# Attention and routed experts in one kernel: split weights held on chip, full tiles listed group by group

## The reference, cut to what matters

```python
x = x + _L0_xattn_ref(_layernorm(x), ctx, ctx, gates..., outnorm_scale)
xf = _layernorm(x).reshape(-1, 256)
top_w, top_i = jax.lax.top_k(softmax(xf @ router_w.T), 2)
comb = (top_w / sum(top_w)) scattered to [n, 8]
h = gelu(einsum('nc,ech->enh', xf, w1), approximate=False)
x = x + einsum('ne,enc->nc', comb, einsum('enh,ehc->enc', h, w2))
```

## Time and profile before

| | us |
|---|---|
| median of 3 executions (lowest, highest) | 728.24 (725.85, 734.26) |
| span of the profiled execution, first to last instruction | 716.1 |
| median less span: start and end that the span leaves out | 12.1 |
| TensorE busy | 616.2 (86% of the span) |
| VectorE, ScalarE, GpSimd busy | 402.2, 299.7, 256.9 |
| moved by DMA | 130.52 MB, mean 182 GB/s |

### The profile page before, as it was taken

One profiled execution on the slowest core, in us unless ns is written; L12 is line 12 of the kernel. 1 busy time (PEld: TensorE's weight loads), 2 busy tenths in 40 slices (PEclk: granted clock), 3 DMA queues, 4 the chain that ended last, 5 costly groups with the idle time before them and its releaser, 6 DMA issues.

```text
span 716.1 us, 18339 instructions
## 1 busy us (share of the span) xinstructions
PE 616.2 (86%) x5879; PEld 498.6 (70%) x5879; DVE 402.2 (56%) x1118; ACT 299.7 (42%) x582; POOL 256.9 (36%) x192
## 2 busy tenths in 40 slices
PE   2799988988999830099999999999999999999991
PEld 2578777776887730078787777777787878777880
DVE  1458678687686655045555555555555555555550
ACT  2444634625444200044545444444544454544440
POOL 0213148568475467012133232233231322312322
PEclk9965657557565555599999999999999999999996
DMA  9786486594541425913944938537649358377321
GB/s 313 272 323 224 173 292 223 208 329 176 196 185 75 177 81 178 367 26 54 343 101 102 349 48 260 179 59 222 218 74 369 56 135 298 52 205 243 48 36 22
DMA packets 58964, 130.52 MB, mean 182 GB/s; under 512 B 6384, under 2 KB 38384, under 8 KB 57904
## 3 DMA queue, kind: packets, MB, share of 16 engines
q1 hardware_dynamic: 44384, 110.91, 43.2%
q0 software_dynamic: 13392, 18.10, 14.1%
q10 hardware_dynamic: 1152, 1.07, 0.4%
HBM read 188.49 MB, written 40.13 MB: 319 GB/s over the span
## 4 chain that ended last, share of the span: by engine, by line
PE 69%; DVE 8%; ACT 6%; issue 5%; DMA 5%; POOL 4%; SPq 2%; POOLq 0%; DVEq 0%; ACTq 0%
PE bank L664 16%; PE bank L650 9%; PE bank L652 9%; PE bank L651 9%; PE bank L666 8%; PE bank L542 6%; PE bank L485 5%; DMA out<-ct,dst 2%; PE bank L634 2%; PE bank L527 2%; POOL rows L1282 2%; ACT xn L695 2%; DMA xrow<-rows 1%; POOL hrs L1274 1%; DVE rowb L874 1%
## 5 line engine op out<-in xcount | busy, mean ns | idle before, releaser
L650 PE MATMUL bank<-dt,wring 128*128 128x128 f16 x1136 | 198.5, 220 | 1.1 <-DVE dt L1201 1.1
L652 PE MATMUL bank<-dt,wring 128*128 128x128 f16 x1136 | 198.6, 220 | 0.0
L651 PE MATMUL bank<-dt,wring 128*128 128x128 f16 x1136 | 198.5, 220 | 0.0
L664 PE MATMUL bank<-wring,ct 128*128 128x512 f16 x568 | 192.3, 379 | 1.3 <-DVE ct L1217 1.3
L1217 DVE TENSOR_TENSOR ct<-dt,ct 128x512 f16<-128x512 f32 x142 | 98.3, 692 | 139.0 <-PE bank L666 113.1
L814 ACT ACTIVATE dt<-bank 128x512 f32<-128x512 f32 x142 | 84.8, 597 | 216.3 <-PE bank L652 216.3
L666 PE MATMUL bank<-wring,ct 128*128 128x256 f16 x568 | 154.8, 273 | 0.0
L1318 POOL DMA_INDIRECT out<-ct,dst x48 | 76.6, 1596 | 211.8 <-DMA out<-ct,dst 75.8
L650 PEld LDWEIGHTS bank<-dt,wring 128*128 128x128 f16 x1136 | 111.3, 98 | 25.1 <-issue 15.7
L651 PEld LDWEIGHTS bank<-dt,wring 128*128 128x128 f16 x1136 | 111.4, 98 | 0.9
L652 PEld LDWEIGHTS bank<-dt,wring 128*128 128x128 f16 x1136 | 111.4, 98 | 0.0
(11 more groups left out here) (139 smaller groups left out, 830.2 us busy)
## 6 DMA issues: line engine op xcount, KB each, us to landing
wring<-wsplit SPq DMA_DIRECT2D x284, 512.0 KB
wring<-in_w SPq DMA_DIRECT2D x16, 1024.0 KB, 12.0
xrow<-rows SPq DMA_DIRECT2D x71, 130.0 KB
wsplit<-wring SPq DMA_DIRECT2D x4, 2048.0 KB, 8.4
wsplit<-wcv SPq DMA_DIRECT2D x4, 2048.0 KB, 7.9
xa<-in_x SPq DMA_DIRECT2D x8, 512.0 KB, 9.1
kT<-in_ctx_t SPq DMA_DIRECT2D x8, 512.0 KB, 8.6
ctn<-in_ctx SPq DMA_DIRECT2D x8, 512.0 KB, 8.4
```

The costliest lines, as they stand in the source:

```text
L650: pe.matmul(o, hi, xT[k][:, c, :], start=(c == 0), stop=False)
L651: pe.matmul(o, hi, xT[k][:, CK + c, :], start=False, stop=False)
L652: mm = pe.matmul(o, lo, xT[k][:, c, :], start=False, stop=(c == CK - 1))
L664: pe.matmul(YP[k][:, 0:2 * D], gh[a][:, m4, :], wring[:, k, w:w + 2 * D], start=(a == 0 and m4 == 0), stop=False, skip_group_check=True)
```

## The change

The split weights of all eight experts lie in `wall` in SBUF; `wsplit`, the ring and its conditional loads are gone. The staging of an expert's fp32 numbers is in the part of `wall` that is not yet written (`first_stage`, `second_stage`). To make room, x isn't kept: it is loaded once for the first norm and again for the residual (`load_x_again`), and most buffers of the attention are single.

The order is new. A step t now has the whole of a group's attention and router in it (`w` = t), beside it `m` = t+1 (decay), `f` = t+2 (x, gates) and `r` = t-1 (ranks, scatter, list). It is cut into eight slots, and a slot may hold a tile: tile i runs in slot 4 of step 2 for i = 0, and so on, so that 44 tiles lie in steps 2 to 7, and 27 behind them. From group 1 on, each routed group gives a list of eight full tiles (`list_step`, 16 small steps on VectorE); the last gives 24 entries, with the ends that aren't full. Everything is unrolled; there is no loop and no value in a register for semaphores. The expert of a tile is taken from a word that packs eight of them, and the weights of each matmul are addressed by it.

Further: `output` has three matmuls of 256 columns in place of 512 and 256, with one sum in PSUM and one bank; ScalarE scales it (`weigh`) and makes the high part of the rows (`tile_high`); the sum on VectorE goes. A ring of three holds finished outputs (`YO`). The second norm goes from VectorE to ScalarE (`x1_norm`), the exponential of the router to GpSimd (`pow`). ScalarE changes its function table twice a step from step 3 on. The pad rows are written by SyncE.

```diff
-SPLIT = {e - 1: (e,) for e in range(NE)}
+SPLIT = {(-2, 7): (0,), (-1, 1): (1,), (-1, 2): (2,), (-1, 4): (3,), (-1, 6): (4,),
+         (0, 0): (5,), (0, 2): (6,), (0, 4): (7,), (0, 5): (8,), (0, 6): (9,), (0, 7): (10,),
+         (1, 0): (11,), (1, 2): (12,), (1, 4): (13,), (1, 6): (14,), (1, 7): (15,)}
...
+def tile_of(step, slot):
+    return PER * (step - 2) + slot - LAG
...
+        wall = sb("wall", [P, NE, 2 * (W1 + W2)], F16)
...
+        def steps(step):
+            for t in range(-2, NG + 1):
+                step(t, group(t), group(t + 1), group(t + 2), group(t - 1))
...
+            def load_rows(i):
+                if i % PER == 0 and i <= PER * (LAST - 1):
+                    sp.wait_ge(s_tab, 2 * (i // PER + 1))
+                    sp.wait_ge(s_sc, 16 * 2 * G * (i // PER + 2))
...
+            def expert(i):
+                if i // PER not in words:
+                    words[i // PER] = pe.value_load(word[0:1, i // PER:i // PER + 1], min_val=0, max_val=8 ** PER - 1)
+                return (words[i // PER] >> (3 * (i % PER))) & (NE - 1)
...
+            def weights(i, at, n):
+                return wall[:, bass.ds(experts[i], 1), at:at + n].rearrange("p o n -> p (o n)")
...
+                    if i == 0:
+                        pe.wait_ge(s_wl, 2 * NE)
+                        pe.wait_ge(s_wh, 2 * NE)
...
+                    experts[i] = pe.snap(expert(i), min_val=0, max_val=NE - 1)
...
+                        hi = weights(i, c * HID + m * P, P)
+                        lo = weights(i, W1 + c * HID + m * P, P)
+                        pe.matmul(o, hi, xT[i % XT][:, c, :], start=(c == 0), stop=False)
+                        pe.matmul(o, hi, xT[i % XT][:, CK + c, :], start=False, stop=False)
+                        mm = pe.matmul(o, lo, xT[i % XT][:, c, :], start=False, stop=(c == CK - 1))
...
-                    pe.matmul(YP[k][:, 0:2 * D], gh[a][:, m4, :], wring[:, k, w:w + 2 * D],
-                              start=(a == 0 and m4 == 0), stop=False, skip_group_check=True)
-                    mm = pe.matmul(YP[k][:, D:2 * D], gl[a][:, m4, :], wring[:, k, w:w + D],
-                                   start=False, stop=(a == 1 and m4 == 3), skip_group_check=True)
+                    pe.matmul(Y, gh[q][:, m4, :], weights(i, w, D), start=(a == 0 and m4 == 0), stop=False)
+                    pe.matmul(Y, gh[q][:, m4, :], weights(i, w + D, D), start=False, stop=False)
+                    mm = pe.matmul(Y, gl[q][:, m4, :], weights(i, w, D), start=False, stop=(a == 1 and m4 == 3))
...
+            def step(t, w, m, f, r):
+                if w is not None:
+                    logd(w, (0, 1, 2))
+                    scores(w, 0)
+                    logd(w, (3,))
+                for j in slots(t):
+                    i = tile_of(t, j)
+                    if live(i):
+                        hidden(i, 0)
+                    if live(i + 1):
+                        tile_turn(i + 1)
+                    if j == 0 and w is not None:
+                        scores(w, 1)
+                    if live(i - 1):
+                        output(i - 1, 0)
+                    if j == 0 and w is not None:
+                        values(w, 0)
...
+                    if j == 4 and f is not None:
+                        turn(f, 0)
+                        turn(f, 1)
+                    if j == 5 and w is not None:
+                        router_turn(w, 0)
+                    if j == 6 and w is not None:
+                        logits(w)
+                    if j == 7 and f is not None:
+                        gates(f)
+                    if live(i):
+                        hidden(i, 1)
+                    if j == 0 and w is not None:
+                        values(w, 1)
+                        values(w, 2)
+                    if live(i - 1):
+                        output(i - 1, 1)
...
+            def weigh(i):
+                act.wait_ge(s_m2, 2 * i + 2)
+                act.wait_ge(s_cw, i + 1)
+                after(act, s_oa, 16 * (i - YO + 1))
+                act.activation(yo[i % YO][:, :], Y, ACT.Copy, scale=cw[i % RW][:, :]).then_inc(s_yo, 1)
...
+                if w is not None:
+                    if t > 2:
+                        act.preload_act_table_set("natural_log_exp_and_others")
+                    floor(w)
+                    for b in range(G):
+                        decay(w, b)
+                if m is not None:
+                    log_sigmoid(m)
+                if w is not None and t > 1:
+                    act.preload_act_table_set("gelu_and_others")
...
+                    if j == 1 and r is not None:
+                        for b in range(G):
+                            scatter(r, b)
```

More of the change, by code:

```diff
@@ L71 @@
 B_MASK = B_IDENT + P
[L72 removed]
+B_TRI = B_MASK + P
 B_ONES = B_TRI + P
@@ L453, in _ @@
-            tiles(sp, tile)
+            load_c(0)
+            for half in range(3):
+                load_w(half)
+            def step(t, w, m, f, r):
+                if t == -2:
+                    load_x(1)
+                    load_x_again(0)
+                    load_k(1)
+                    for half in range(3, 7):
+                        load_w(half)
+                if t == -1:
+                    load_x(2)
+                    load_c(1)
+                    for half in range(7, 12):
+                        load_w(half)
+                    sp.dma_start(rows[SPARE:SPARE + P, :], pad_rows).then_inc(s_spare, 16)
+                    sp.dma_start(out[NT:NT + P, :], pad_rows[:, 0:D]).then_inc(s_spare, 16)
+                if t == 0:
+                    load_k(2)
+                    for half in range(12, 2 * NE):
+                        load_w(half)
+                if t == 1:
+                    load_x_again(1)
+                if t > 0 and f is not None:
+                    load_x(f)
+                for j in slots(t):
+                    i = tile_of(t, j)
+                    if live(i + 2):
+                        if i + 2 == PER * (LAST - 1):
+                            sp.wait_ge(s_pr, 1)
+                            for e in range(NE):
+                                pad_rows_of(e)
+                        load_rows(i + 2)
+                    if j == 0 and t > 0 and f is not None:
+                        load_k(f)
+                    if j == 1 and t > 1 and w is not None:
+                        load_x_again(w)
+                    if j == 3 and t >= 0 and f is not None:
+                        load_c(m + 1)
+                    if j == 4 and w is not None:
+                        store_x1(w)
@@ L454, in _ @@
+            steps(step)
             sp.wait_ge(s_oa, 16 * TILES)
+            sp.wait_ge(s_x1o, 16 * NG)
         @block.tensor
@@ L796, in _ @@
-            groups(step)
-            act.wait_ge(s_pr, 1)
-            act.wait_ge(s_prep, 16)
-            for e in range(NE):
-                r = act.value_load(padr[0:1, e:e + 1], min_val=e * REGION, max_val=e * REGION + NT)
-                act.dma_start(rows[bass.ds(r, P), :], pad[:, :]).then_inc(s_pad, 16)
-            act.wait_ge(s_prepg, 4)
-            act.wait_ge(s_n, 5 * NG)
-            act.activation(en[0][:, 0:1], mhalf[:, 0:1], ACT.Gelu)
-            HPS, YP = [D0, D1], [K0, K1, UB]
```

1102 lines of the change are left out of this document (539 added, 563 removed).

## The result

The changed kernel takes 820.64 us (median of 3 runs, 820.47 to 820.64) against 728.24: a ratio of 1.124, with a 95% interval from 1.117 to 1.132. Ratios compare fast executions alone with fast ones, while a median may hold slower ones, so a ratio and a difference of medians needn't agree exactly. The profiled execution has a span of 818.7 us, 1.9 under the median. The change costs 92 us by the medians; the forecast was 774 us, 46 more than before.

The account below looks back on a forecast made before the run. TensorE bound the old tiles; register addresses were to make its sequencer the limit. First tile 158 + step 2 attention 10 + later attention 115 + tiles 469 + end 10 = 762, with 12.1 around the span 774 us; range 685 to 950.

Parts of the forecast that it names:

- The side: Whole kernel: slower than before, 774 us against 728.24, 6%; chance of slower 0.70, of faster by over 1% 0.24.
- register operations cost nothing: Rival for the tiles: addresses fit beside the array's work, the tile keeps 5.46 us, 693 us in all; chance 20%.
- nothing is shared: Rival for the tiles: an address is made anew at each use, 72 operations, 8.9 us a tile, 937 us; chance 21%.
- the clock falls in the tiles: Rival for the tiles: TensorE is granted 1.2 GHz, 10.9 us a tile, 1079 us in all; chance 9%.
- a register operation takes a place of about 95 ns, an instruction 8: TensorE's sequencer in the tiles: 48 operations at 95 ns and 148 instructions at 8 ns, within 6.6 us a tile.
- The third rival's mechanism, handing over beside operations: Rival for the tiles: the queue takes the 144 instructions while register operations run, 724 us, no change; chance 10%.
- The first tile: Time before the tiles: first tile at 158 us, between 140 and 180, with 46 us a step for steps 0 and 1.
- the chain "43 us": Before the first tile: a group's chain from decay matrix to ranks, 49 us in the old kernel's last group, less about 6.
- GpSimd at nothing: Beside the tiles: GpSimd busy 54 to 60 of 76 us a step; `weigh` waiting for output places costed at nothing.
- Beside the tiles: Steps with tiles: attention is added, 23 us a step, 115 for five steps and 10 in step 2; 76 us a step.
- The 4 us of idle time: At a step's start: TensorE idles about 4 us before `scores`, while ScalarE loads a table and makes two decays.
- 12.1 us: Whole kernel: time taken to lie around a span, added to the 762 us of span to give 774 us.

Follow-up runs that it names:

- e1: The changed kernel with each tile taking a fixed expert's weights, so no matmul has an address in a register: 746.79 us, ratio 1.033 to the kernel before.
- e9: The changed kernel with byte addresses made four at a time in one fused register operation ahead of use, 12 a tile instead of 48: 751.8 us, ratio 1.055.
- e2: The changed kernel with a second register for the second matmul on each high half, so 72 register operations a tile instead of 48: 1014.73 us, ratio 1.402.
- e5: The changed kernel with weights read through a byte view, each address one plain addition instead of a fused operation, still 48 a tile: 791.6 us, ratio 1.094.
- e8: The changed kernel with all tiles on expert 0 at a static address and the splits of halves 5 to 15 left out: 737.03 us, measured once.
- e12: e11 with GpSimd's input-norm power directly behind the head norm's, and VectorE's next-tile low half and row weights ahead of shifts and residual: 714.4 us, ratio 0.990.
- e6: The changed kernel with VectorE's next-tile low half and row weights ahead of the head norm in slot 2, GpSimd's centring behind its power: 809.75 us, ratio 1.117.
- e11: e9 with VectorE's slot 2 reordered, ScalarE's input norm behind the tile's halves, and in step 1 GpSimd's power ahead of the scatters: 732.7 us, ratio 1.008.

## Why the prediction was right or wrong

**The side: right, for the reason given.** TensorE's sequencer sets the pace of the tiles with one operation for each different address, 48 a tile, and a static matmul needs none. e1 and e9 show it from two sides: no operations, or a quarter of them, and the tile is at 5.5 us. The rival "register operations cost nothing" is refuted, "nothing is shared" as well (e2 built it, and it is dearer than its 8.9 us). So is "the clock falls in the tiles": it is 1.00 in the late ones. (What was said against that rival was misread in part: the decay matrix's matmuls have 512 columns.) It did fall between them: behind the gates, as the forecast had it, and, not foreseen, behind the stop before slot 3.

**The price of an operation: the term that was mis-sized.** The step "a register operation takes a place of about 95 ns, an instruction 8" was right only in its sum, 238 against 248 ns. It took the place from operations at a loop's edge, which follow one another directly: there 60 ns pass between two records, and this reading was right. In the tiles weight loads and matmuls follow each operation, and then 78 to 80 pass, so that a fused one has 124 and a plain one 112 (e5). The 8 ns an instruction are not there: 2, 4 or 12 between cost the same (e2, after, e9). What the 48 of the earlier trace rows cost beside an operation was not tested. The third rival's mechanism, handing over beside operations, was therefore there, but brought no gain, because the 95 ns were short by as much. The Trainium skill, "Advanced Engine Details and Errata" (Sequencer Loop), has it that other engine instructions can be read and queued while a control instruction executes; by b = 0 these traces agree. Over 71 tiles the term is 511 us instead of 469: +42.

**The first tile: the forecast's own bound, 180 us, was passed.** 198.7 against 158: step 0 starts 6 us late, steps 0 and 1 are 25 longer together, step 2's part is 10 longer. Of this 3 us are splits (13 instead of 10, e8), and 8 us were won back by e12's orders. The step that failed is the chain "43 us" taken from the last group: there nothing stood in the queues but a neighbour's scatters and logits, here every piece of the next group is interleaved with it, and TensorE spends 71 of the first 200 us in three kinds of wait. The other 30 us weren't separated by a run, and their cause stays open.

**GpSimd at nothing: right where it was looked for, wrong elsewhere.** ScalarE's `weigh` never waited for a place for outputs in the trace (its 35.4 us of waits all end with a matmul of L656), and TensorE waited 0.8 us in all for `weigh`, so the term that was put at nothing was nothing. GpSimd is busy 149 of the 384 us in which attention lies between tiles, so it isn't short of time either. But its order carries a chain that the prediction has nowhere: scatters, centring, power, head norm. How busy an engine is says nothing of who waits behind it.

**Beside the tiles: right in the sum, not in the parts.** 78.4 us a step against 76, with dearer tiles (57.6 against 52.8) and less attention (20.8 against 23). "Attention isn't hidden under tiles, it is added" is not quite so: it is added for the array, but the sequencer seems to gain its lead there, as e1's step of 71.6 and the nearly unchanged slots 0 and 1 suggest. The 4 us of idle time were expected at `scores`; there it was 1.4, and 4.9 stood before slot 3, behind the head norm, with 6.8 us of the lower clock behind them. In all, attention and idle time beside tiles are 607 - 511 = 96 us between the first tile's start and 7.2 us after the last one's (805.5 - 198.7 = 607), against 125. That the two misses of a step nearly cancel is luck.

**The sum.** 774 + 41 (first tile) + 42 (tiles) - 29 (96 against 125 beside them) + 3 (end) - 10 (1.9 instead of 12.1 us around the span) = 821. The range was wide enough; two errors of 40 us had the same sign. The last term is no behaviour of the new kernel but the 12.1 us that should have been 1.9.

## What to carry to other kernels

Before matmuls are given addresses in registers, count the different addresses and compare the sequencer's sum with the array's; then make several addresses in one fused operation ahead of their use, for it is the number of operations that costs, their steps little (9 ns for a record of four additions against one of three steps), and the register in the matmul nothing that was seen. When a group's work is interleaved with other work on in-order queues, look in each slot at what each engine's first waiting instruction blocks: the piece that TensorE wants next must stand ahead of any piece that waits for a slow neighbour. Moving one piece wins less than the wait that it ends, because the next piece stands behind the same wait, and a step forward for one (the power) can be a step back for another (the scatters). Look at the granted clock behind a stop as well, for the stop can cost more than its length.

## What the runs showed of the hardware that was not expected

- A register operation on TensorE's sequencer takes 78 to 80 ns more than its record when weight loads and matmuls follow it, be it 2, 4 or 12 of them (46 ns: 124; 32 ns: 112; 55 ns, four additions: 133), and 60 ns more when the next operation follows directly (36 ns: 96).
- Late in a stop of 4.9 us and behind it TensorE was granted 1.2 GHz, for 6.8 us (421.4 to 428.2 us in the kernel after).
- VectorE's operations last longer beside GpSimd's centring; the centring itself doesn't (1.91 us in step 1 and here). In the kernel after an operation on 8 elements a partition, where its neighbours in the list take 0.2 us, took 2.51 while the centring ran (412.09 to 414.00 us), here in VectorE's timeline:
```profile
411.53 2.51 DVE L1146 SCALAR_TENSOR_TENSOR ad<-adr,dn,cst 128x8 f32<-128x8 f32 x1
```
The head norm takes 1.22 us in all eight groups of the kernel after and 2.9 in seven of e6's eight, where the centring was moved behind the power. In step 2 of e11 both can be seen side by side: the head norm from 190.54 us for 2.92, the centring from 190.49 to 192.38 us. It is a cost of e6's order that wasn't in its expectation.
